# A transformer layer on eight cores: the residual loads and stores of the output projection issued from ScalarE's queue instead of GpSimd's

## The reference

```python
x = x + attn(layernorm(x), Wqkv, b_qkv, Wout, b_out)
x = x + ffn(layernorm(x), gate_w, gate_scale, up_w, up_scale, down_w, down_scale)
...
# attn: 32 heads of 64, rotary on the first 32 features of q and k, causal softmax
scores = einsum('bthd,bshd->bhts', q, k * scale)
attn = softmax(where(causal_mask, -10000.0, scores))
out = einsum('bhts,bshd->bthd', attn, v).reshape(B, S, D)
return out @ Wout + b_out
...
# ffn: 8-bit weights with a scale for each output row
h = silu(g) * u
return einsum('bsi,hi->bsh', h, Wd)
```

## Time and profile before

| | us |
|---|---|
| runs shown | 5450.52 and 5634.77, median 5542.64 |
| profiled execution | 5426.09, span of its slowest core (core 3) 5424.2 |
| spans of the eight cores | 5387.0 to 5424.2, granted clock 0.919 to 0.923 |
| heads 4 to 15 of query groups 1, 2, 3 | 227.0, 259.6, 318.2 |
| last 16 units, without attention | 118.6 |
| third stage, from 2570 us on | 2854.2 |

### The profile page before, as it was taken

How to read it: one execution, slowest core, us unless ns; L and a number is a source line. 1 busy time by engine, 2 the same in 40 slices (tenths; PEclk the granted TensorE clock), 3 DMA queues, 4 the chain that set the end, 5 groups by cost and what they waited for, 6 DMA issues and landing times.

```text
span 5424.2 us, 60072 instructions; the slowest of 8 cores (5387.0 to 5424.2 us)
## 1 busy us (share of the span) xinstructions
PE 4616.0 (85%) x21072; PEld 2009.4 (37%) x21072; DVE 1805.2 (33%) x2637; ACT 1107.2 (20%) x1395; POOL 1997.9 (37%) x3784
## 2 busy tenths in 40 slices
PE   4668989954777878854999989999899998999998
PEld 2323333321232323322444444444444444444443
DVE  4645552144544443322333212332123332133301
ACT  1200000033556687631111100111001110011100
POOL 1011011001112221122656455665456655566654
PEclk8779999965788999977999999999999999999999
DMA  4233234313445554444556566665666656666655
GB/s 97 69 71 58 45 57 62 50 48 68 93 103 104 114 117 95 95 94 124 149 147 154 149 175 167 151 152 137 174 184 152 151 136 171 171 155 150 151 146 155
DMA packets 768745, 656.39 MB, mean 121 GB/s; under 512 B 266416, under 2 KB 731456, under 8 KB 764224
## 3 DMA queue, kind: packets, MB, share of 16 engines
q0 software_dynamic: 522592, 503.77, 40.2%
q1 hardware_dynamic: 236640, 132.00, 9.5%
q10 hardware_dynamic: 9216, 16.78, 0.8%
HBM read 446.53 MB, written 58.98 MB: 93 GB/s over the span
## 4 chain that ended last, share of the span: by engine, by line
PE 49%; DMA 2%; DVE 1%; POOL 1%; issue 0%; ACT 0%; DVEq 0%; ACTq 0%; SPq 0%; POOLq 0%
PE pu L826 16%; PE pg L826 16%; PE pg L920 8%; PE pu L920 8%; PE psh L875 1%; DMA out<-outst 1%; POOL wgub L97 1%; DMA wgub<-wd_t 1%; DVE outst L944 0%; DMA wgub<-wu_t 0%; DVE outst L948 0%; PE psh L778 0%; PE ptp L763 0%; DMA x1buf<-x_scr 0%; DVE stats L201 0%
## 5 line engine op out<-in xcount | busy, mean ns | idle before, releaser
L826 PE MATMUL pg<-xn2f,wgub 128*128 128x512 bf16 x4096 | 901.8, 381 | 20.7 <-DVE gl L834 14.7
L826 PE MATMUL pu<-xn2f,wgub 128*128 128x512 bf16 x4096 | 894.5, 379 | 0.8 <-DMA wgub<-wu_t 0.8
L316 PE MATMUL pq<-wbuf,xnf 128*128 128x512 bf16 x3072 | 747.4, 400 | 78.0 <-DVE xnf L301 43.1
L97 POOL DMA_DIRECT2D wgub<-wd_t x1024 | 540.9, 600 | 493.2 <-PE pu L920 375.1
L97 POOL DMA_DIRECT2D wgub<-wg_t x1024 | 540.8, 601 | 411.3 <-PE pg L826 353.8
L97 POOL DMA_DIRECT2D wgub<-wu_t x1024 | 540.9, 602 | 349.8 <-PE pu L826 301.2
L826 PEld LDWEIGHTS pg<-xn2f,wgub 128*128 128x128 bf16 x4096 | 402.0, 98 | 511.0 <-issue 35.0
L826 PEld LDWEIGHTS pu<-xn2f,wgub 128*128 128x128 bf16 x4096 | 400.2, 98 | 485.2 <-issue 3.6
L839 ACT ACTIVATE sil<-gl,gs_sb 128x512 f32<-128x512 f32 x256 | 184.5, 722 | 1514.5 <-DVE gl L834 1514.4
L598 DVE RECIPROCAL rdbuf<-oc 1x512 bf16<-1x512 f32 x128 | 428.0, 3344 | 145.5 <-ACT oc L583 134.2
L920 PE MATMUL pg<-wgub,h_sb 128*128 128x512 bf16 x2048 | 459.3, 383 | 16.0 <-DVE outst L948 12.4
(11 more groups left out here) (91 smaller groups left out, 3614.8 us busy)
## 6 DMA issues: line engine op xcount, KB each, us to landing
wgub<-wg_t POOLq DMA_DIRECT2D x1024, 128.0 KB, 2.4
wgub<-wu_t POOLq DMA_DIRECT2D x1024, 128.0 KB, 2.4
wgub<-wd_t POOLq DMA_DIRECT2D x1024, 128.0 KB, 2.4
wobuf<-wout POOLq DMA_DIRECT2D x256, 128.0 KB, 8.6
wbuf<-wqkv POOLq DMA_DIRECT2D x192, 128.0 KB, 8.8
xbuf<-x SPq DMA_DIRECT2D x16, 1024.0 KB, 5.2
xresb<-x POOLq DMA_DIRECT2D x64, 256.0 KB, 3.6
x_scr<-o1st POOLq DMA_DIRECT2D x64, 256.0 KB, 3.3
```

The source lines that it names most:

```text
L97: return emit(e, lambda eng, o=out_ap, i=in_ap: eng.dma_start(o, i), ctr)
L316: emit("tensor", lambda e, d=dcc, t=tt, w=wslot, p=par: e.matmul(pq[p][:, :], xnf[:, d, t * P:(t + 1) * P], wbuf[:, w, d, :], start=(d == ...
L826: mmv = emit("tensor", lambda e, d=dcc, i=icl, s=slot, ps=ps: e.matmul(ps[:, :], wgub[:, s, d, i * P:(i + 1) * P], xn2f[:, d, :], start=(d ...
```

## The change

In `wout_unit` the load of `xresb`, the wait for the add and the store of `o1st` move from GpSimd's list to ScalarE's. That is 64 loads and 64 stores of 256 KB in all. Nothing else moves; the lists of TensorE and VectorE are word for word the same.

```diff
                 xsl = u % 2
-                rwait("gpsimd", xres_rel[xsl])
-                xr = dma("gpsimd", xresb[:, xsl, :],
+                rwait("scalar", xres_rel[xsl])
+                xr = dma("scalar", xresb[:, xsl, :],
                          dx[qg * 512 + ts * P: qg * 512 + (ts + 1) * P,
                             og * 512:(og + 1) * 512], ldxr[xsl])
...
                 xres_rel[xsl] = (ev, o1v)
-                wait("gpsimd", ev, o1v)
-                sv = dma("gpsimd",
+                wait("scalar", ev, o1v)
+                sv = dma("scalar",
                          x1_scr[qg * 512 + ts * P: qg * 512 + (ts + 1) * P,
                                 og * 512:(og + 1) * 512],
                          o1st[:, osl, :], stx1[osl])
```

## The result

The changed kernel takes 5799.28 us in the median of 11 runs (5681.88 to 6330.1), the kernel before 5546.03 us in the median of 10 (5430.76 to 6079.87).

What follows compares the result with a forecast made beforehand. Bound by ScalarE's pace after tile 4 in group 3, VectorE's chain in groups 1 and 2. 72 + 74 + 49 + 10 + 54 - 13 - 15 - 26 = +205: 5631 profiled, 5655 reported; range 5545 to 5780.

Steps and rivals of the forecast that it cites:

- ScalarE waits for the add: In 36 heads tile 4 stands behind the store, in group 3 at 16.0 us instead of 9.82; +72, +74, +49, +10 us.
- The rival that the exponentials are not held: In the 36 heads activations run on past the waiting store and heads stay as they are; 5389 us, chance 0.06.
- The second load: In two-unit heads, issued behind the first store, landing after 3.6 us; tile 4 starts at 20.8 us instead of 15.1.
- TensorE's clock: TensorE's stop of some 8 us before tile 4 costs 1.5 us in each of 36 heads: +54, ends 0 and +65.
- The rival of the lasting low clock: TensorE stays at 1.2 GHz through the rest of each head, about 4.5 us a head, +108: 5763 us, chance 0.18.
- GpSimd's queue is freed: 128 issues and 64 waits fewer: between groups 1 and 2 -13, wait ahead of last units -15, last 16 units -26.
- The chain gets shorter: Rival: with GpSimd's list empty the round trip is 3 us shorter in 36 heads; +97, 5547 us, chance 0.07.
- the last step: 24 us added to the profiled 5631, since the profiled execution lay 24.4 below the lower run shown; gives 5655.

Runs made afterwards that it cites:

- the deferred store: The changed kernel, but within heads the store and its wait stand behind the head's last exponential in ScalarE's list; ratio to the kernel before 0.9934.
- the run with the chain late: The changed kernel, but in heads with units the chain of the softmax sums stands behind the adds in VectorE's list; ratio to the kernel before 1.0109.

## Why the prediction was right and wrong

*ScalarE waits for the add.* Right, to the digit in the place where it was read off: 16.04 us to tile 4 in group 3 against 16.0, and 20.2 to 20.9 in two-unit heads other than head 6 against 20.8. The rival that the exponentials are not held fell with the first head. The place in the list is shown to be the cause by the deferred store, and the chain ahead of the add by the run with the chain late. VectorE was idle ahead of its reciprocals in group 1 too, as foretold. That the rows of groups 1 and 3 come out within 2 us (+76.7 against +77, +88.2 against +90) is in part luck: two-unit heads were up to 1 us shorter than forecast, and head 6 was 3 to 4 us longer.

*The second load.* The 3.6 us were close (3.3), but one of the steps failed where it was not applied: I let loads of `x` share the DMA engines with weight loads only in the last units. In head 6 of each group the second load is under way with the 16 weight loads, and that head is 4.7, 8 and 4 us longer than the other two-unit heads, some 16 us together, of which 3 in group 2 are the slower round trip.

*TensorE's clock.* This step failed in size: 54 us stood in the sum, 74 were measured behind tile 4, above the forecast's upper end of 65. "I take 1.5, between 0 and 1.8" rested on one unit after one stop, a stretch where TensorE was back at full speed by the next unit. In the heads that did not hold: the clock stayed low to the copy in groups 1 and 2 and came back only in group 3. The price was 1.0, 3.9 and 1.3 us a head. It was small in group 1, where only the diagonal tiles stand behind the stop. So a stop is to be priced over all the work behind it. The rival of the lasting low clock was right about the clock in 24 of 36 heads, and near its price of 4.5 us a head in the 12 of group 2; over all 36 that price was too high, 162 against 74. Filling the stop takes the 4 us back. Why the clock comes back in group 3 and not in the other two is open: the stops of its one-unit heads, 4.9 to 9.0 us, are not shorter than the 5.3 to 7.8 of group 2 (heads 4 aside), where "some 8 us" were forecast.

*GpSimd's queue is freed.* -13.4 against -15, -22.5 against -26, -15.9 against -20. From add to add it was 4.2 to 5.5 us in the last seven units against 4.75, and up to 9.0 beside weight loads. One bound was that only the time of issuing is saved, -17, which is also what the rule of the Trainium skill would make of it ("DMA: Bandwidth & Descriptors", "Issuing engines are not separate DMA queues"). For the sharing of the DMA engines the trace agrees with that rule: the second load of head 6 took 8.7 us beside weight loads instead of 3.1 to 3.5. As the bound of what a move can give it does not hold here: with the load alone moved the last units became 35 us shorter, twice the 17, since the load then stands behind no weight loads and no store that waits. In the changed kernel a store with its wait still stands ahead of each load, which leaves 22.5.

*The chain gets shorter* fell: L616 waited 5.64 us for the round trip, as before (5.65), with nothing else in GpSimd's list.

*The number.* The profiled execution came to 5682 where the working had 5631; the forecast's own ends were 5542 and 5696 on that scale, so the working was within its bounds, 51 us low. The larger part of the miss is the last step, "so I add 24 at the end". The reported 5799 is a median over all executions, and it lies 117 us above the profiled one; I had carried the scale over with 24, from the lower of the two runs shown. That the median shown was 117 us above the profiled execution stood in the text and was not used. That is 93 us too little beside the working's 51, and the range missed by 19: either fault alone would have left the time within it. The 93 say nothing about the change: in the result the median of the kernel before lies as far, 120 us, above its profiled execution (5546 against 5426).

## What to carry to other kernels

A wait moved to another engine's list is priced by what stands behind it there and by what stands ahead of the awaited instruction in its own list: here some 6 us ahead of key tile 4 in each of 36 heads, because an add that nobody needed soon stood behind a 15 us chain, and 1 to 4 us more behind it through the clock. A transfer that waits for a late result belongs in a list with nothing urgent behind it, or at a later place of the same list. A transfer that waits for nothing gains where it gets out from behind waits, as the load did in ScalarE's list, and loses where it gets behind one, as in SyncE's. Where a new stop of TensorE comes in, look at what it does to the clock in all the work after it, and not in the next few matmuls.

## What the runs showed of the hardware

After a stop of 6.4 us the granted clock was 0.54 over the next 15 us in a head of group 2, with TensorE busy 12.3 of them. After one of 4.9 us in a head of group 3 it was back at full about 6.5 us after tile 4, and after longer stops in that group, up to 9.0 us, it came back before the head's end too (0.74 or more over the stretch). With 6.2 us of otherwise useless matmuls in the stop it was 1.00 to the end of six of the seven one-unit heads from head 5 on in group 2, and these took 3.3 to 5.4 us less.

The 256 KB load of `x` landed 3.3 us after its issue from ScalarE's queue and 3.6 from GpSimd's, the store 2.3 against 3.3; beside 16 weight loads the load took 8.7 us to the add instead of 3.1 to 3.5. An issue takes 0.33 us of ScalarE's list and 0.55 of GpSimd's, and in the deferred run it went beside a running exponential.
